# A decoder layer's projection stage: every second tile's value product put off, the row norm on ScalarE, the ones of the key table written last

## The reference

```python
xn = _layernorm(_layernorm(x), ln_gamma, ln_beta)
q, k, v = proj(w_q), proj(w_k), proj(w_v)       # 8 heads of 64
qn = _rmsnorm(q, q_gamma) * dh ** (-0.5)
kn = _rmsnorm(k, k_gamma)
attn = softmax(einsum('bhid,bhjd->bhij', qn, kn))
out = einsum('bhij,bhjd->bhid', attn, v)
```

## Time and profile before

| | |
|---|---|
| time, median of 3 runs | 2322.66 us (2322.13 to 2323.05) |
| the profiled execution's own time | 2315.09 us |
| its span, first to last instruction | 2313.3 us |
| granted TensorE clock, mean | 0.992 |
| TensorE busy | 2178.3 us, 94% |
| VectorE, ScalarE, GpSimd busy | 1552.2, 1612.0, 1542.5 us |

### The profile page before, as it was taken

The page is one execution under the profiler, slowest core; times in us unless marked ns, Lnnn a source line. Parts: engine busy times, 40 slices in busy tenths (PEclk is TensorE's granted clock), DMA queues, the critical chain, the costliest instruction groups (busy, mean ns, idle before and its releaser), DMA issues. The chain is left out here.

```text
span 2313.3 us, 62611 instructions
## 1 busy us (share of the span) xinstructions
PE 2178.3 (94%) x22392; PEld 1254.6 (54%) x22392; DVE 1552.2 (67%) x2573; ACT 1612.0 (70%) x1831; POOL 1542.5 (67%) x1008
## 2 busy tenths in 40 slices
PE   6988999999997989899989899999999978998999
PEld 3544666666665455444445456666666644554444
DVE  5897777777776666753368977777777767667532
ACT  3556999999998556731145579999999975566210
POOL 5644988989988577721246368998989976867210
PEclk9999999999999999999999999999999999999999
DMA  4220000000001301103112100000000022021000
GB/s 105 56 49 3 4 7 9 9 9 9 9 0 28 100 6 39 46 12 81 46 51 56 42 1 10 0 9 9 9 9 9 9 61 64 2 47 38 19 23 33
DMA packets 102348, 65.23 MB, mean 28 GB/s; under 512 B 75346, under 2 KB 75346, under 8 KB 102226
## 3 DMA queue, kind: packets, MB, share of 16 engines
q1 hardware_dynamic: 102226, 63.57, 12.5%
HBM read 46.69 MB, written 8.39 MB: 24 GB/s over the span
## 5 line engine op out<-in xcount | busy, mean ns | idle before, releaser
L597 POOL TENSOR_TENSOR qkn<-wide 128x1024 f16<-128x1024 f32 x448 | 986.7, 2234 | 136.5 <-PE bank L710 120.7
L909 DVE TENSOR_REDUCE sq<-bank 128x1 f32<-128x512 f32 x1024 | 679.8, 688 | 246.8 <-PE bank L666 244.1
L836 ACT ACTIVATE wide<-bank,shift 128x1024 f32<-128x1024 f32 x512 | 571.0, 1115 | 37.3 <-DVE qkn L923 30.7
L828 ACT ACTIVATE wide<-bank,shift 128x1024 f16<-128x1024 f32 x512 | 568.1, 1110 | 9.9 <-PE bank L682 9.9
L681 PE MATMUL bank<-q_hh,ko 128*128 (+1 forms) x1024 | 388.9, 380 | 18.5 <-ACT wide L836 13.6
L666 PE MATMUL bank<-ko,q_hh 128*128 (+1 forms) x1024 | 387.7, 380 | 10.7 <-DVE sq L909 7.1
L682 PE MATMUL bank<-q_lm,k_h 65*128 (+1 forms) x1024 | 389.0, 380 | 0.0
L695 PEld LDWEIGHTS bank<-v_hl,wide 128*128 128x128 f16 x4096 | 287.6, 98 | 63.4 <-issue 5.7
L695 PE MATMUL bank<-v_hl,wide 128*128 (+1 forms) x4096 | 320.0, 192 | 0.1
L697 PE MATMUL bank<-v_hl,wide 128*128 (+1 forms) x4096 | 318.1, 193 | 0.0
L697 PEld LDWEIGHTS bank<-v_hl,wide 128*128 128x128 f16 x4096 | 267.5, 96 | 58.7
(11 more groups left out here) (228 smaller groups left out, 4213.2 us busy)
## 6 DMA issues: line engine op xcount, KB each, us to landing
wide<-in_x SPq DMA_DIRECT2D x32, 256.0 KB, 2.7
q_lm<-in_x SPq DMA_DIRECT2D x32, 256.0 KB, 3.2
ko<-in_L_ffn_W SPq DMA_DIRECT2D x32, 256.0 KB, 4.1
q_hh<-q_hh SPq DMA_DIRECT2D x32, 128.0 KB, 2.6
ko<-k_h SPq DMA_DIRECT2D x32, 128.0 KB, 2.8
out<-bo_b SPq DMA_DIRECT2D x16, 256.0 KB, 2.0
out<-xbo_b SPq DMA_DIRECT2D x16, 256.0 KB, 2.0
q_lm<-sq SPq DMA_DIRECT2D x248, 0.2 KB, 4.9
```

Of the source, the lines that this page charges most:

```text
L597: pool.tensor_tensor(probs_l[:, p % 2, :], probs[:, p % 2, :], probs_h[:, p % 4, :], ALU.subtract).then_inc(pl_pool, 1)
L828: act.activation(probs_h[:, p % 4, :], SB[p % 2][:, :], ACT.Exp, bias=shift[:, 0:1]).then_inc(ph_ready, 1)
L836: act.activation(probs[:, p % 2, :], SB[p % 2][:, :], ACT.Exp, bias=shift[:, 0:1]).then_inc(p_ready, 1)
L909: dve.tensor_reduce(pm[:, s, k:k + 1], MB[k % 2], AX_X, ALU.max).then_inc(mx_free, 1)
```

## The change

Five edits, all in the projection stage and the start of the attention stage:

1. The tiles whose value products are put off are now the eight odd ones, not the last seven. Values are made in the order 0, 2, ..., 14, 1, 3, ..., 15 (`VALUES`), and the semaphores of the values count in this order (`v_turn`).
2. The norm of row tiles 2 to 15 moves from GpSimd to ScalarE, between the high part of turned rows t + 1 and the square of the keys of t. GpSimd gets a third small instruction, the offset (`row_offset`), with a semaphore of its own, `a_nb`. Tiles 0 and 1 are as they were.
3. The memset of the ones of the key table moves from the end of step 0 to the end of step 13, behind the last row's affine.
4. Four put-off tiles are left when the maxima start, where three were: four tiles run behind the steps as before, three beside the first 18 maxima, and the eighth in halves of six matmuls, one ahead of the row's turning and one behind it. Its high part on ScalarE comes behind the copy of the row, its low part on VectorE before maximum 5 of block 1.
5. The waits for all values and for the ones beside the values move from ahead of the first scores to ahead of the first value product of unit 0; ahead of the scores stand waits for the first seven put-off tiles and the ones of the keys.

```diff
-        def row_normalise(eng, b, t, s, first=False):
+        def row_offset(pool, b, t, s):
+            pool.wait_ge(a_rs, b * KB + t + 1)
+            pool.nop(nofuse=True)
+            pool.tensor_scalar(rows_rs[:, 2, s:s + 1], rows_mv[:, s, 0:1], rows_rs[:, 1, s:s + 1], -1.0, ALU.mult, ALU.mult)\
+                .then_inc(a_nb, 1)
+
+        def row_normalise_scalar(act, b, t, s):
+            T0 = b * KB
+            act.wait_ge(a_nb, b * (KB - 2) + t - 1)
+            act.wait_ge(a_t_done, T0 + t - 1)
+            act.activation(rows_n[:, s, :], rows_in[:, s, :], ACT.Identity, bias=rows_rs[:, 2, s:s + 1],
+                           scale=rows_rs[:, 1, s:s + 1]).then_inc(a_y, 1)
...
-                    LATE = 7
-                    FIRST_LATE = KB - LATE
+                    LATE = range(1, KB, 2)
+                    VALUES = [*range(0, KB, 2), *LATE]
...
-                        return banks[2] if t >= FIRST_LATE and (t - FIRST_LATE) % 2 else banks[7]
+                        return banks[2] if t in LATE and LATE.index(t) % 2 == 0 else banks[7]
...
                         def ones():
-                            pool.wait_ge(a_xn, T0 + 3)
+                            pool.wait_ge(a_xn, T0 + KB)
...
                             if next2:
                                 row_scale(pool, b, t + 2, s)
-                                row_normalise(pool, b, t + 2, s)
+                                row_offset(pool, b, t + 2, s)
                                 row_affine(pool, b, t + 2, s)
-                            if not before:
+                            if t == KB - 3:
                                 ones()
...
-                            if t < FIRST_LATE:
+                            if t not in LATE:
-                                pe.wait_ge(a_v_ready, T0 + t + 1)
+                                pe.wait_ge(a_v_ready, v_turn(t) + 1)
...
                         def values_high(u, p, ob):
                             pe.wait_ge(ph_ready, (U0 + u) * PAIRS + p + 1)
+                            if isinstance(u, int) and u == 0 and p == 0:
+                                pe.wait_ge(a_v_ready, T0 + KB + 1)
+                                pe.wait_ge(a_ones, 2 * b + 2)
...
                         for k in range(18):
                             unit_max(k // 16, k % 16)
                             late_values(4 * V + 2 * k, 4 * V + 2 * k + 2)
+                        late_values(7 * V, 7 * V + V // 2)
...
                         mm.then_inc(e_row, 1)
+                        late_values(7 * V + V // 2, 8 * V)
                         for k in range(2, AHEAD):
                             unit_max(1, k)
-                        pe.wait_ge(a_ones, 2 * b + 2)
-                        pe.wait_ge(a_v_ready, T0 + KB + 1)
+                        pe.wait_ge(a_ones, 2 * b + 1)
+                        pe.wait_ge(a_v_ready, T0 + KB)
                         scores(0, 0, fresh=True)
...
                             square(t, 0, QB[s], a_q_done)
                             if next1:
                                 row_high(act, b, t + 1, turned(t + 1)[0])
+                            if next2:
+                                row_normalise_scalar(act, b, t + 2, s)
                             square(t, 1, KBK[s], a_k_done)
...
                         act.activation(lf[DH:DH + 1, 0:CT], OB[0][DH:DH + 1, :], ACT.Copy).then_inc(m_ready, ROW)
+                        v_high(LATE[7])
...
                         for k in range(AHEAD):
-                            if k == 2:
-                                v_low(KB - 1)
+                            if k in (2, 5):
+                                v_low(LATE[6 if k == 2 else 7])
                             reduce_max(1, k, 1)
```

More of the change, by code:

```diff
@@ L122, in decoder_layer @@
         rows_mv = sb(top, "mv_a", [P, 2, 2], F32)
-        rows_rs = sb(top, "rs_a", [P, 2, 2], F32)
+        rows_rs = sb(top, "rs_a", [P, 3, 2], F32)
         wide32 = sb(top, "wide32", [P, 4 * D], F32)
@@ L200, in decoder_layer @@
         a_rs = sem("a_rs")
+        a_nb = sem("a_nb")
         a_y = sem("a_y")
@@ L335, in row_scale, with row_normalise @@
                 .then_inc(a_rs, 1)
-        def row_normalise(eng, b, t, s, first=False):
-            T0 = b * KB
[L339 to L343, removed]
+        def row_offset(pool, b, t, s):
[4 more added lines that the diff above has]
+        def row_normalise_scalar(act, b, t, s):
+            T0 = b * KB
+            act.wait_ge(a_nb, b * (KB - 2) + t - 1)
+            act.wait_ge(a_t_done, T0 + t - 1)
+            act.activation(rows_n[:, s, :], rows_in[:, s, :], ACT.Identity, bias=rows_rs[:, 2, s:s + 1],
+                           scale=rows_rs[:, 1, s:s + 1]).then_inc(a_y, 1)
+        def row_normalise(dve, b, t, s):
+            T0 = b * KB
+            dve.wait_ge(a_rs, T0 + t + 1)
+            dve.tensor_scalar(rows_n[:, s, :], rows_in[:, s, :], rows_mv[:, s, 0:1], rows_rs[:, 1, s:s + 1],
                               ALU.subtract, ALU.mult).then_inc(a_y, 1)
@@ L421, in _ @@
                 row_stats(dve, 0, 0, 0)
-                row_normalise(dve, 0, 0, 0, first=True)
+                row_normalise(dve, 0, 0, 0)
                 split_low(dve, 0, PIECES_P1[:1], stage1, *wq_of)
@@ L426, in _ @@
                 split_low(dve, 0, PIECES_P1[1:2], stage1, *wq_of)
-                row_normalise(dve, 0, 1, 1, first=True)
+                row_normalise(dve, 0, 1, 1)
                 dve.wait_ge(s_pool, 4)
@@ L504, in turned, with v_turn @@
                     def turned(t):
-                        return (late[t][:, 0, :], late[t][:, 1, :]) if t >= FIRST_LATE else                             (rows_h[:, t % 2, :], rows_l[:, t % 2, :])
+                        return (late[t][:, 0, :], late[t][:, 1, :]) if t in LATE else                             (rows_h[:, t % 2, :], rows_l[:, t % 2, :])
                     def v_bank(t):
-                        return banks[2] if t >= FIRST_LATE and (t - FIRST_LATE) % 2 else banks[7]
+                        return banks[2] if t in LATE and LATE.index(t) % 2 == 0 else banks[7]
+                    def v_turn(t):
+                        return T0 + VALUES.index(t)
                     block = ph.enter_context(nc.Block())
@@ L610, in late_values @@
                             for i in range(first, last):
-                                t, d, kind = FIRST_LATE + i // (3 * DC), i // 3 % DC, i % 3
+                                t, d, kind = LATE[i // (3 * DC)], i // 3 % DC, i % 3
                                 if i % (3 * DC) == 0:
-                                    pe.wait_ge(a_v_ready, T0 + t + (1 if t == FIRST_LATE else 0))
+                                    pe.wait_ge(a_v_ready, v_turn(t))
                                 xh, xl = turned(t)
@@ L795, in v_high @@
                         def v_high(t):
-                            act.wait_ge(a_v_done, T0 + t + 1)
+                            act.wait_ge(a_v_done, v_turn(t) + 1)
                             act.activation(v_tile(t, False), v_bank(t)[:, :].rearrange("p (h d) -> p h d", d=DH), ACT.Copy,
@@ L815, in _ @@
                         act.preload_act_table(ACT.Exp)
-                        v_high(FIRST_LATE)
-                        v_high(FIRST_LATE + 1)
+                        v_high(LATE[0])
+                        v_high(LATE[1])
                         heads_high(KB - 1)
-                        for t in range(FIRST_LATE + 2, KB):
+                        for t in LATE[2:7]:
                             v_high(t)
@@ L877, in v_low @@
                         def v_low(t):
-                            dve.wait_ge(a_vh, T0 + t + 1)
+                            dve.wait_ge(a_vh, v_turn(t) + 1)
                             dve.scalar_tensor_tensor(out=v_tile(t, True), in0=v_bank(t)[:, :].rearrange("p (h d) -> p h d", d=DH),
@@ L898, in _ @@
                             step(t, t % 2, t > 0, t + 1 < KB, t + 2 < KB)
-                        v_low(FIRST_LATE)
-                        v_low(FIRST_LATE + 1)
+                        v_low(LATE[0])
+                        v_low(LATE[1])
                         heads_low(KB - 1)
-                        v_low(FIRST_LATE + 2)
+                        v_low(LATE[2])
                         def reduce_max(r, k, s):
@@ L965, in _ @@
                         dve.tensor_copy(eye16[:, :], ident[:, :]).then_inc(e_eye, 1)
-                        v_low(FIRST_LATE + 3)
+                        v_low(LATE[3])
                         for k in range(16):
@@ L969, in _ @@
                             if k in (7, 13):
-                                v_low(FIRST_LATE + (4 if k == 7 else 5))
+                                v_low(LATE[4 if k == 7 else 5])
                         dve.wait_ge(e_zero, b + 1)
@@ L2568, in _ @@
                                             row_stats(dve, b + 1, j, j)
-                                            row_normalise(dve, b + 1, j, j, first=True)
```

(1 more changed line is left out.)

## The result

The changed kernel takes 2343.01 us (median of 4 runs, 2341.01 to 2346.21) against 2322.39 us (4 runs, 2320.96 to 2323.05): a ratio of 1.0091, 95% interval 1.0073 to 1.0108. Its profiled execution took 2342.44 us, a span of 2340.7.

What follows compares the result with a forecast made beforehand. TensorE was taken as near full, with time lost to a memset gap, VectorE-led late steps and a stretched small maximum. The terms, (9.9 + 1.8) x 2 batches = 23.4 us, added to 2322.66, gave 2346.1; range 2328 to 2351.

Steps and rivals of the forecast that it cites:

- A step after the change: Projection steps: ScalarE's norm ahead of the key square delays VectorE's second sum; even steps 9.78 us, odd 9.19, pair 18.97.
- S: Start of a projection step on VectorE: its first instruction, the statistics of tile t + 2.
- rival of a hidden norm: Projection steps: ScalarE's square comes no later than today, a pair falls to 15.63 us, kernel 2306 us; chance 0.10.
- The clock falls in every pair: Rival, projection steps: TensorE's idle in odd steps lowers its clock, even steps 10.9 us, kernel 2362 us; chance 0.04.
- The gap in step 2: Early projection: the memset ahead of the norms idles TensorE; moving it cuts step 2 from 14.67 to 9.78 us.
- The memset's new place: Step 13: GpSimd's memset holds VectorE's small maximum to its end, so step 14 starts 5.3 us later.
- no lock: Rival, step 13: the memset does not stop VectorE's small maximum; 9.4 us slower, 2332 us; chance 0.19.
- The end of the steps: After step 13: TensorE idles 5 us, lower clock costs 1.7; tile 14's head transposes at 171.6, 9.9 us late.
- The eighth tile: Before the first scores: 12 products of the eighth put-off tile, 2.59 us, make the scores 1.8 us late.
- The sum: Whole kernel: (9.9 + 1.8) x 2 batches = 23.4 us slower, 2346.1 us.

Runs made afterwards that it cites:

- e5: e1 (changed kernel, memset last) with the norm back on GpSimd, every second tile still put off; 2306.36 us, ratio 0.9937 to the kernel before.
- e6: e1 with the norm still on ScalarE, but VectorE making a row tile's statistics earlier, ahead of the heads' scaling; 2292.18 us, ratio 0.9878 to the kernel before.
- e3: Kernel before with one edit of the change alone, the memset at the end of step 13; 2310.11 us, ratio 0.9954 to the kernel before.
- e1: Changed kernel with the memset of the key table's ones after the last small maximum (tile 15); 2327.65 us, ratio 1.0033 to the kernel before.
- e2: Changed kernel with the same memset at the same place cut into 16 parts of 512 words; 2328.92 us, ratio 1.0036 to the kernel before.
- e10: e8 with seven odd tiles put off (3 to 15) instead of eight; 2294.47 us, ratio 0.9894 to the kernel before.
- e8: e5 with the statistics early: norm on GpSimd, memset last, every second tile put off; 2293.01 us, ratio 0.9878 to the kernel before.
- e9: Kernel before with memset last and statistics early, the last seven tiles put off, norm on GpSimd; 2301.72 us, ratio 0.9922 to the kernel before.

## Why the prediction was right, step by step

- **A step after the change.** Forecast: the sum starts at S + 3.80, steps of 9.78 and 9.19. Measured: S + 3.75 or 3.76 (98.66 to 102.42, 146.16 to 149.91), 9.74 and 9.14. Two of the chain's links came from a norm of a later stage of the same kernel, the others from step 11, and each held within 0.03 us: 1.14 to GpSimd's first instruction, 1.29 from there to the norm, 0.72 to the square. The rival of a hidden norm is refuted by e5 and e6 together: the norm costs nothing on ScalarE when its input is early, and when it is not, VectorE waits 1.62 us in each step, and a pair takes 18.88 us instead of 16.87 (e5). *The clock falls in every pair* did not come either: the granted clock is 1.00 in each window of 10 us from 90 to 150, with 7.57 to 9.15 us of TensorE's work in it.
- **The gap in step 2.** Gone, as forecast; step 2 lasts 9.74 us. e3 shows the gap's worth by itself, 5.6 us a batch.
- **The memset's new place.** Forecast 5.3 us a batch from L862, measured 5.4; e1 and e2 show that it is the exclusion and that it lasts for one instruction of GpSimd. The rival "no lock" is refuted. The Trainium skill (SBUF — State Buffer, "Who interferes with whom") says that of a VectorE instruction in a two-port mode and a GpSimd instruction the one that issues first has the shared ports for its whole length, and the other is blocked. The trace agrees, for a GpSimd instruction that only writes: 5.57 us for 0.17, to 0.03 us after the memset. In which mode L888 runs no run here shows.
- **The end of the steps.** The size of one term was off: the lower clock cost 2.8 us (8.64 us in e1, 11.43 with it), where 1.7 was taken and called an upper bound. It was at 0.50 behind an idle of 4.84 us, and the head transposes were slow too, not only the products. The forecast start of tile 14's transposes, 171.6, still met the measured 171.67 by luck: step 14 had started 0.7 us earlier than forecast (160.70 for 161.4), since step 2 had started 0.65 earlier than the 42.31 assumed, and this offset most of what the clock took beyond its term.
- **The eighth tile.** Forecast 1.8 us; from the first maximum to the first scores it is 17.31 us (184.81 to 202.12) where it was 15.70, 1.6 more. In e10, without it, it is 15.51.
- **The sum.** 11.7 us a batch forecast, 11.67 read at the first scores of the first batch. So close a match is partly the luck of the offset errors. In the second batch it is 11.7 as well (176.7 against 165.0). The medians give 20.6 instead of 23.4, with 17 to 25 as interval. The stage of the first batch counted from its first sum is 12.2 us longer, since the stage's start itself differs from execution to execution (the first sum starts between 25.5 and 28.8 us in the twelve profiles). That the stage accounts for more than the medians do stays within what the medians can tell; where the rest is was not followed up. A slip without weight: the prediction counts 26 norm steps in its bounds, but the norms of tiles 2 to 15 are 28 in two batches.

What the forecast did not say is what the parts are worth by themselves. By the medians, e3 puts the memset's move at 11 us less; e5, which adds the alternation with its eighth tile, at 14 less, so that 3 to 4 us fall to the alternation, which is within the intervals. The norm on ScalarE then costs 21 us (e1 against e5), and the memset in step 13 beside it 15 more (the changed kernel against e1), though the same place costs nothing in e3. The alternation, which carries the change's name, pays clearly only once the statistics are early: 7 to 9 us (e8 and e10 against e9).

## What to carry to other kernels

When work moves to an engine with room, look not at its busy share but at what stands behind it in that engine's order and when its input comes: 0.7 us of work ahead of a critical square made a wait of 1.6 us and a step 1.0 us longer, and the same work at the same place cost nothing once its input was made 1.7 us earlier on another engine (the statistics start 2.59 us ahead of the step's first sum in e6, 0.88 in e1). A long instruction of GpSimd should be cut into parts or placed by what VectorE does beside it: the same memset cost 5.4 us, 0.4 or nothing by its place and its length. And a gap that is closed is to be weighed by itself: here it alone was worth 11 us of the two batches' time, and the change hid it.

## What the runs showed of the hardware

A GpSimd memset on one partition, which reads nothing, blocked VectorE's small maximum of 128 x 16 float32 words, from SBUF to SBUF, to the memset's end: 5.57 us for 0.17. It did not slow the low parts of the heads, which read PSUM and SBUF: 1.51 us. In 16 instructions the same memset takes 7.54 us, 9% more than the 6.92, and blocked for 0.39 us. TensorE's granted clock was 0.50, its lower level (1.2 of 2.4 GHz), behind an idle of 4.84 us, for head transposes and nine products, and this cost 2.8 us. On ScalarE the instruction behind a norm starts 0.72 us after the norm's start, while the norm takes 0.81; behind a square from PSUM, 0.58 us long, it is 0.48.
